# A diffusion transformer with 16 images on one core: loop heads moved to slot 0 of an instruction fetch block, and back-edge hints on the short loops

## The reference

```
x: (16, 256, 128)   ctx: (16, 1601, 128)   cond: (16, 128)
a0, c1, c2:  q = LN(x) Wq;  k, v = ctx' Wk, ctx' Wv;  x += softmax(q k^T / sqrt(8)) v Wp
             (ctx' = LN(ctx) in a0 and c2, ctx as it is in c1)
s1, s2:      the same, with k and v from the modulated LN(x), and a gate on the result
m1, m2:      x += gate * (gelu(mod(LN(x)) W1 + b1) W2 + b2)
l3:          evidence = softmax(q (ctx Wk)^T / sqrt(128)) ctx Wv, three experts, router, gate
```

## Time and profile before

| | |
|---|---|
| median of 3 runs | 6722.88 us (6714.82 to 6731.32) |
| time of the profiled execution | 6733.98 us |
| its span in the profile | 6732.2 us |
| TensorE busy | 6088.2 us, 90% of the span |
| ScalarE, VectorE, GpSimd busy | 4247.2, 4124.3, 985.3 us |
| granted TensorE clock, mean | 0.967 of full speed |
| a pass of the a0 loop, mean of 13 | 98.45 us |
| a pass of the c1 loop | 95.00 to 101.52 us, mean of 13 98.90 |
| a pass of the c2 loop, mean of 13 | 97.52 us |

### The profile page before, as it was taken

The page is one execution under the profiler, slowest core; times in us unless marked ns, Lnnn a source line. Parts: engine busy times, 40 slices in busy tenths (PEclk is TensorE's granted clock), DMA queues, the critical chain, the costliest instruction groups (busy, mean ns, idle before and its releaser), DMA issues.

```text
span 6732.2 us, 147754 instructions
## 1 busy us (share of the span) xinstructions
PE 6088.2 (90%) x49714; PEld 3143.3 (47%) x49714; DVE 4124.3 (61%) x6520; ACT 4247.2 (63%) x8158; POOL 985.3 (15%) x1660
## 2 busy tenths in 40 slices
PE   6999999999777999999999677699999999979998
PEld 3444444444444444444444344344444444435554
DVE  5767777776555666666666255467777776624332
ACT  3777777777665776776677366477777777732222
POOL 3112112211111111111110011122112211100000
PEclk9999999999998999999999899899999999989998
DMA  2222222221112222222231011222232222101110
GB/s 85 75 69 62 63 76 66 56 74 43 58 58 71 78 68 56 76 70 57 71 78 35 17 57 57 64 67 64 68 78 68 56 75 76 38 32 41 42 43 23
DMA packets 181115, 405.58 MB, mean 60 GB/s; under 512 B 16992, under 2 KB 124560, under 8 KB 166416
## 3 DMA queue, kind: packets, MB, share of 16 engines
q1 hardware_dynamic: 180752, 400.01, 22.1%
HBM read 316.81 MB, written 83.14 MB: 59 GB/s over the span
## 4 chain that ended last, share of the span: by engine, by line
PE 73%; issue 8%; DVE 8%; ACT 7%; DMA 2%; SPq 1%; POOL 1%; ACTq 0%; DVEq 0%; POOLq 0%
PE bank L1058 18%; PE bank L1104 18%; PE pair L1074 14%; DVE MX L1400 3%; PE bank L1030 2%; ACT P L1234 2%; PE bank L645 2%; PE bank L1025 2%; PE bank L636 2%; PE pair L1091 1%; DMA QP<-scr_q 1%; PE pair L1080 1%; ACT QP L1245 1%; PE pair L574 1%; DVE ST L1357 1%
## 5 line engine op out<-in xcount | busy, mean ns | idle before, releaser
L1234 ACT ACTIVATE P<-bank 128x512 f32<-128x512 f32 (+1 forms) x5504 | 3104.0, 597 | 1415.4 <-PE bank L1058 1375.1
L1400 DVE TENSOR_REDUCE MX<-pair 128x2 f32<-128x802 f32 x3072 | 2923.9, 988 | 1367.4 <-PE pair L1074 1359.8
L1058 PE MATMUL bank<-QP,KP 128*128 128x256 bf16 (+1 forms) x11008 | 2097.0, 277 | 155.3 <-ACT P L1234 100.2
L1104 PE MATMUL bank<-P,VA 128*25 128x256 f32 (+1 forms) x22016 | 1769.7, 392 | 38.2 <-issue 32.8
L1074 PE MATMUL pair<-KP,QP 96*128 96x401 bf16 x6144 | 1582.8, 339 | 60.3 <-DMA QP<-scr_q 42.0
L1058 PEld LDWEIGHTS bank<-QP,KP 128*128 128x128 bf16 (+1 forms) x11008 | 859.3, 100 | 1598.6 <-ACT P L1234 917.4
L1104 PEld LDWEIGHTS bank<-P,VA 128*25 128x25 f32 (+1 forms) x22016 | 403.6, 102 | 751.7 <-issue 497.2
L1074 PEld LDWEIGHTS pair<-KP,QP 96*128 96x128 bf16 x6144 | 595.3, 99 | 184.1 <-DVE MX L1400 64.0
L1404 DVE TENSOR_REDUCE MX<-pair 128x4 f32<-128x1024 f32 x256 | 311.3, 1223 | 327.2 <-PE pair L1080 326.5
L1525 POOL COPY VA<-VN 128x416 f32<-128x416 f32 (+1 forms) x320 | 139.2, 436 | 2533.6 <-PE bank L1104 2452.1
L1245 ACT CAST QP<-pair 2x512 bf16<-2x512 f32 x640 | 339.5, 576 | 130.1 <-PE pair L1091 124.6
(11 more groups left out here) (213 smaller groups left out, 4611.1 us busy)
## 6 DMA issues: line engine op xcount, KB each, us to landing
KP<-scr_k SPq DMA_DIRECT2D x192, 900.6 KB
QP<-scr_q SPq DMA_DIRECT2D x960, 48.0 KB
CN<-ctx_n SPq DMA_DIRECT2D x40, 768.0 KB
scr_k<-KSF SPq DMA_DIRECT2D x48, 600.8 KB, 3.2
scr_k<-KSF SPq DMA_DIRECT2D x48, 600.0 KB, 3.2
CT<-ctx_t SPq DMA_DIRECT2D x24, 800.5 KB, 4.5
KP<-scr_ks SPq DMA_DIRECT2D x128, 144.0 KB
scr_q<-QS SPq DMA_DIRECT2D x80, 192.0 KB, 2.1
```

The lines of the kernel that those rows point to most:

```text
L1058: last = nc.tensor.matmul(SC[half][0:kt, k * N:(k + 1) * N], KP[g][:, c0:c0 + kt], QP[g][:, h * N:(h + 1) * N], start=True, stop=True)
L1104: last = nc.tensor.matmul(OB[32 * h:32 * h + STEP + HD + 1, 0:N], VA[g % 2][0:kt, t, h, :], P[(g * ph.nt + t) % 2][0:kt, h * N:(h + 1) * N ...
L1234: nc.scalar.activation(P[v % 2][0:kt, half * 2 * N:(half + 1) * 2 * N], SC[half][0:kt, :], ACT.Exp, scale=SCALE).then_inc(sem("probs_full" ...
L1400: nc.vector.tensor_reduce(MX[:, r, c:c + 2], MP[j % 2][:, :].rearrange("p (t k) -> p t k", t=2)[:, :, 0:SPANS[0][1]], AX.X, ALU.max).then_ ...
```

## The change

A helper `loop` takes the place of every `Fori`. It asks for the hint in each of them, also in those that had none, and for the head of each loop at slot 0 of a fetch block of the engine's instructions. For this the code in front of a head gets padding, and a taken branch over it. It is done on every engine: on TensorE, ScalarE and VectorE eleven loops each, on GpSimd five, on SyncE six.

```diff
+        def loop(eng, first, end):
+            return nc.Fori(first, end, engines=[eng.engine], hint_back_edge=True, head_slot={eng.engine: 0})
...
         def mlp_tensor(pe, ph):
             at = ph.c.at
             stream_ready(pe, before(ph))
-            with pe.Fori(0, B // 4) as q:
+            with loop(pe, 0, B // 4) as q:
...
-    def run(self, engine, step, experts):
+    def run(self, engine, loop, step, experts):
...
-        with engine.Fori(1, B // 2 - 1) as i:
+        with loop(engine, 1, B // 2 - 1) as i:
...
                     element(ph.el["first"])
-                    with nc.Fori(1, B - 1, engines=[pe.engine], hint_back_edge=True) as i:
+                    with loop(pe, 1, B - 1) as i:
                         element(ph.el["middle"](i))
```

More of the change, by code:

```diff
@@ L440, in mlp_tensor @@
                         sem("mlp_var"), 1)
-            with pe.Fori(0, B // 2) as i:
+            with loop(pe, 0, B // 2) as i:
                 pe.wait_ge(sem("mlp_normed"), at("mlp_normed", B // 2 - 1, 1))
@@ L455, in mlp_scalar @@
             at = ph.c.at
-            with act.Fori(0, B // 4) as q:
+            with loop(act, 0, B // 4) as q:
                 for k in range(2):
@@ L466, in mlp_scalar @@
             nc.scalar.preload_act_table(ACT.Gelu_apprx_tanh)
-            with act.Fori(0, B // 2) as i:
+            with loop(act, 0, B // 2) as i:
                 for c in range(4):
@@ L475, in mlp_vector @@
             at = ph.c.at
-            with dve.Fori(0, B // 4) as q:
+            with loop(dve, 0, B // 4) as q:
                 for k in range(2):
@@ L490, in mlp_vector @@
                 dve.wait_ge(sem("mlp_normed"), at("mlp_normed", q * 2, 2))
-            with dve.Fori(0, B // 2) as i:
+            with loop(dve, 0, B // 2) as i:
                 dve.wait_ge(sem("mlp_out"), at("mlp_out", i, 1))
@@ L528, in last_sync @@
                 load(2 + r, r)
-            with sp.Fori(1, B // 2 - 1) as i:
+            with loop(sp, 1, B // 2 - 1) as i:
                 for r in range(2):
@@ L680, in last_tensor @@
             rows(0, 0)
-            ph.run(pe, step, experts)
+            ph.run(pe, loop, step, experts)
             for t in range(len(CROSS_TILES)):
@@ L745, in experts @@
                 nc.scalar.preload_act_table_set(LN_EXP)
-            with act.Fori(0, B // 4) as q:
+            with loop(act, 0, B // 4) as q:
                 norms(q)
             row(0, 0)
-            ph.run(act, step, experts)
+            ph.run(act, loop, step, experts)
             for t in range(len(CROSS_TILES)):
@@ L901, in last_vector @@
             shifts(0, 0)
-            ph.run(dve, step, experts)
+            ph.run(dve, loop, step, experts)
             for t in range(len(CROSS_TILES)):
@@ L965, in _ @@
                     prepare(ph.el["first"])
-                    with nc.Fori(1, B - 1, engines=[sp.engine], hint_back_edge=True) as i:
+                    with loop(sp, 1, B - 1) as i:
                         prepare(ph.el["middle"](i))
@@ L1280, in _ @@
                     element(ph.el["first"])
-                    with nc.Fori(1, B - 1, engines=[act.engine], hint_back_edge=True) as i:
+                    with loop(act, 1, B - 1) as i:
                         element(ph.el["middle"](i))
@@ L1454, in _ @@
                     element(ph.el["first"])
-                    with nc.Fori(1, B - 1, engines=[dve.engine], hint_back_edge=True) as i:
+                    with loop(dve, 1, B - 1) as i:
                         element(ph.el["middle"](i))
@@ L1547, in _ @@
                     element(ph.el["first"])
-                    with nc.Fori(1, B - 1, engines=[pool.engine], hint_back_edge=True) as i:
+                    with loop(pool, 1, B - 1) as i:
                         element(ph.el["middle"](i))
```

## The result

The changed kernel takes 6664.19 us (median of four runs, 6655.6 to 6669.21), the kernel before 6726.41 us beside it (four runs, 6714.82 to 6731.32): ratio 0.9909, 95% interval 0.9891 to 0.9926. That is 62 us, 0.9% faster. The profiled execution took 6661.25 us.

The account below looks back on a forecast made before the run. TensorE, busy 90% of the span, bounds the kernel; only issue waits from refetching c1's nine-block body could move. 6733.98 - 70.3 + 8.0 + 0.5 = 6672.2 us, range 6654 to 6697 for 8 in 10.

Parts of the forecast that it names:

- c1, -70.3: TensorE's long loop c1: 13 passes without instruction fetches fall from 1285.74 to 1215.4 us, 93.49 each.
- c2, 0, at most -3: TensorE's long loop c2: its nine fetches a pass cost next to nothing, so removing them gives 0, at most 3 us.
- Nine blocks don't stay, eight do: TensorE's long loops: bodies in nine 256-instruction blocks are fetched anew each pass (c1, c2), in eight never (a0).
- TensorE's entries, 0: Branches into TensorE's eleven loops: straight code has already fetched the target block; 0, at most 3.86 us each.
- ScalarE's entries, five at 1.6, +8.0: ScalarE's heads of s1, c1, s2, c2 and `run`: fetch on demand takes 1.9 us, 1.6 shows each; +8.0 us.
- my list of targets: ScalarE's heads whose branch lands beyond the next half block: five long ones, and short loops except m1's and m2's first.
- Hints, +0.5: Short loops: one more instruction per pass and engine is hidden except in the norm loops; +0.5 us, uncovered 7.6.
- one or two more long passes of c1: Why the profiled execution was 11.1 us above the median: a pass or two more of c1's long kind, 6.5 each.
- 6.5 us on each of eleven heads: Rival: every taken branch into a loop lands in an absent block, also on TensorE; eleven cost 72 us; chance 0.07.
- half cleared: Rival in c1 and c2: fetching behind the loop pushes the first block out, two packets a pass remain; 6696 us, chance 0.06.
- nothing changed: Rival: the change makes no difference to the time; chance 0.08.

Follow-up runs that it names:

- c1_only: Kernel before, with only TensorE's head of the c1 loop placed at slot 0; 6647.89 us, ratio 0.9883.
- pe_att: Kernel before, with TensorE's heads of the five attention loops at slot 0, other engines and short loops untouched; 6648.93 us, ratio 0.9886.
- others_only: Changed kernel with TensorE's loops left as before; the other engines keep all heads at slot 0 and all hints; 6737.82 us, ratio 1.0018.
- c1_act: c1_only plus ScalarE's heads of the five attention loops at slot 0; 6653.99 us.
- hints_only: Changed kernel with no head placed, so only the hints of the short loops are added; 6724.54 us, ratio 0.9997.
- slots_b: Changed kernel with TensorE's heads at other slots: a0 128, s1 80, c1 144, s2 80, c2 186; 6776.12 us in one run.
- slots_c: Changed kernel with TensorE's heads at other slots: a0 210, s1 50, c1 160, s2 50, c2 111; 6745.48 us in one run.
- nohint_slots: Changed kernel without the hint in TensorE's attention loops, its c1 and c2 heads at slot 210, the others at 0; 6915.76 us in one run.

## Why the prediction was right

The forecast was 6672, the time 6664.19, inside 6654 to 6697. The main step, the fetches of c1's ninth block and their price, is what the runs show. By its own steps:

- *c1, -70.3:* measured -70.0 in the changed kernel, -70.2 in c1_only. The pass worked out as 93.49 us is 93.48 to 93.55, at clock 1.00, with no packet. Shown as the cause by c1_only (one head, 79 us) and by c1 at 144 and 160.
- *c2, 0, at most -3:* -0.7. The reason given (90 instructions in the last block, and not 36) holds for the first wait: the duration of the back edge's branch follows that number in the 12 hinted loops of nine blocks. It doesn't give the price of a pass by itself; the second packet and the length of the first block come in, as above.
- *Nine blocks don't stay, eight do:* right as far as the hint is there, which I hadn't tied to it. With the hint a0, c1 and c2 run over eight blocks with 0 packets, and without one the loop of `run`, 604 instructions and so at least three blocks, does too. Only the long body without the hint is fetched at its back edge, with 117 packets in a0 and 3.3 to 3.9 us in each branch. The size of 256 instructions was my estimate, from 243 a packet at least and 16.4 KB each; with it, c1 at 144 (2042 slots, 0 packets) and at 160 (2058, 117) show the eight blocks from both sides.
- *TensorE's entries, 0:* right within what can be told; pe_att is 1 us over c1_only, with ranges that overlap. That straight code fetches a block ahead shows in the traces. In the kernel before, the stretch with 17 packets has a single wait of TensorE's matmuls for issue, of 0.2 us. In the changed kernel the taken branch at each of TensorE's eleven heads takes 0.30 to 0.42 us, against 2.9 to 3.5 us at the back edges whose packet starts 0.5 to 1.2 us behind them; the last q8 packet starts 3.7 us or more ahead of it, and the next 0.97 to 1.57 us behind it. Only at s1 in pe_att, where the last packet starts 1.2 us ahead, does the branch take 1.64 us.
- *ScalarE's entries, five at 1.6, +8.0:* the sum is about right, its parts are not. others_only prices the whole of the other engines at 11 to 12 us. The delay that I took as 1.9 us is 2.4 to 3.6, and 4.5 at `run`; at the first loops of m1 and m2 it is 0.4, the two short loops that my list of targets had left out. Of the five heads two show for certain: s2 with about 2 us, `run` with 4.9, 7.1 and 12.7 over c1_only in three kernels. s1 shows 2.7 in c1_act but nothing clear over all kernels, and at c1 and c2 the delay of 2.6 us is hidden. q14 has 45 packets more, as expected. That ScalarE's packets are on q14, and of 8 KB, c1_act shows: over c1_only it places five heads of ScalarE and nothing else, and q14 has 54 packets and 0.44 MB instead of 46 and 0.38, with 81 on q8 in both. That a head's code is not there yet at the branch shows there too: the hint comes 2.5 to 3.3 us behind it, and at a0, c1, s2 and c2 a q14 packet starts 0.9 to 1.3 us behind it. That the target lies one half block further on was my count from the lengths of the program; the 0.4 us at just the two heads that it left out agrees with it.
- *Hints, +0.5:* -2.4 us with an interval from -9 to +4: nothing.
- *The term that was missing:* the stop behind s2's end, -6.2 in the profiles. It was in the trace of before, outside the long loops, where I hadn't looked for waits for issue.
- *Why the profiled execution lay above the median:* I put its 11 us down to one or two more long passes of c1. That fell. The median of 23 runs of the kernel before is 6726.94, so it was 7 us; and hints_only, profiled at 6719.27, has eight passes over 100 us in c1 as the kernel before has, and 1284.53 us in the 13 against 1285.74. Its other 13.5 us are spread over a0 to the last phase in pieces of 1 to 3. What sets them stays open.

From the median of 23 runs the terms as measured give 6726.9 - 70.0 - 6.2 - 0.7 + 11.5 = 6661.5, beside 6664.19. That the forecast was 8 us off, and not more, is partly luck. I carried the profiled execution's sum over as the median, 7.0 us too high at the start; the missing stop was 6.2 more; against them stand the entries with some 3 us more than I took, and 2.7 us that no term explains.

The rivals: entries were dearer than my term at `run` but nowhere near 6.5 us on each of eleven heads; half cleared and nothing changed are excluded by 0 packets in c1 and c2. The mechanism of half cleared, a fetch behind the loop that evicts its head, may be what happens without the hint, there with nine packets in a0 and not two.

## What to carry to other kernels

A loop whose body nearly fills what the engine can hold (on TensorE here eight blocks, 2042 of 2048 slots) is placed by its length plus its head's slot: count the blocks, compare instruction packets between the back edges of loops of like length, and read the duration of the back edge itself and the stop that may follow it at the end of the first block. Place only the heads that need it: here one head of 44 gave 79 us, and the change with all 44 gave 62. Look behind the ends of loops too; a body that ended 12 to 14 slots ahead of a block's end cost a stop of 2.4 to 3.8 us once here, and moving a head moves all ends behind it.

## What the runs showed of the hardware

- TensorE kept eight blocks, taken as 256 instructions or one packet of 16.4 KB each, across a hinted back edge (slots_b, c1: 2042 of 2048 slots used, 0 packets) and none of nine (slots_c, c1: 2058, 9 packets a pass). Without a hint it kept 438 and 604 instructions (nohint_slots and the kernel before, 0 packets), not 1927 in eight blocks (nohint_slots, 9 a pass).
- The back edge took 0.22 us in place, 0.34 to 0.67 us in a nine-block body with 79 to 90 instructions in the last block, 2.9 to 3.5 us with 10 or fewer, 3.3 to 3.9 us for these long bodies without a hint. In c1 of the kernel before a second stop, up to 4.1 us long, came where the next packet started 6.9 to 7.4 us behind the back edge; in the nine-block bodies of a0 and c2 that were cheap it started 1.0 to 1.8 us behind.
- In the changed kernel the branch at a placed head took 0.30 to 0.42 us on TensorE. From that branch to the loop's hint, ScalarE took 2.4 to 3.6 us, 4.5 us at `run` and 0.4 us at the first loops of m1 and m2; VectorE took 2.8 to 3.1 us at ten of its eleven heads and 0.6 at c1's.
- Runs of c1_only lie within 1.4 us of one another, those of the kernel before within 22. In c1_only all passes of one long loop are equal to 0.1 us. c1_act and the changed kernel scatter by 12 and 14 us though their long loops are as even; which of the entries does that isn't shown.
